# A transformer layer on one core: the pairs of scores as words of the plan, every engine's step in another order, and a chain of roots for each norm

## What is computed

```
h = segm_table[seg] + pos + token_table[tok]
x = layernorm(h)
q, k, v = split(x @ qkv_weight.T)              # 12 heads of 16
q = layer_norm(q) * 16 ** -0.5 ; k = layer_norm(k)
attn = softmax(einsum('bhnd,bhmd->bhnm', q, k))
h = h + (attn @ v) @ proj_weight.T
y = layernorm(h)
xq = round(clip(y / mean(alpha_a1), -8, 7)) ; wq1 = round(clip(w1 / alpha_w1, -8, 7))
x1 = clip(gelu(xq @ wq1.T * alpha_w1 * mean(alpha_a1) + b1), -10, 10)
hq = round(clip(x1 / mean(alpha_a2), -8, 7)) ; wq2 = round(clip(w2 / alpha_w2, -8, 7))
h = h + hq @ wq2.T * alpha_w2 * mean(alpha_a2) + b2
```

## Time and profile before

| | |
|---|---|
| median of 3 runs | 1070.74 us |
| lowest, highest | 1069.35, 1071.54 us |
| span of the profiled execution | 1067.6 us |
| PE busy | 979.4 us (92%) |
| ACT busy | 872.6 us (82%) |
| DVE busy | 813.9 us (76%) |
| POOL busy | 411.8 us (39%) |

### The profile page before, as it was taken

One profiled execution on the slowest core, in us unless ns is written; L12 is line 12 of the kernel. 1 busy time (PEld: TensorE's weight loads), 2 busy tenths in 40 slices (PEclk: granted clock), 3 DMA queues, 4 the chain that ended last, 5 costly groups with the idle time before them and its releaser, 6 DMA issues.

```text
span 1067.6 us, 19577 instructions
## 1 busy us (share of the span) xinstructions
PE 979.4 (92%) x7571; PEld 389.1 (36%) x7571; DVE 813.9 (76%) x2325; ACT 872.6 (82%) x950; POOL 411.8 (39%) x345
## 2 busy tenths in 40 slices
PE   5589999999999999999999999999999999989885
PEld 4333433334342433434343343434334343413223
DVE  5878869788686969878696977869697886825347
ACT  1387788897979889797988979798888989798883
POOL 6555513635343353534435363443526412201000
PEclk9899999999999999999999999999999999999997
DMA  7511200303011040202102040110202000000000
GB/s 162 127 16 16 31 1 2 46 1 64 12 25 22 1 75 1 38 8 58 18 2 45 1 73 3 31 16 16 30 1 45 1 16 1 16 1 1 16 1 31
DMA packets 25762, 28.62 MB, mean 27 GB/s; under 512 B 5027, under 2 KB 22182, under 8 KB 25670
## 3 DMA queue, kind: packets, MB, share of 16 engines
q0 software_dynamic: 16896, 11.80, 9.4%
q1 hardware_dynamic: 8624, 15.55, 4.8%
q10 hardware_dynamic: 150, 0.01, 0.0%
HBM read 21.06 MB, written 6.29 MB: 26 GB/s over the span
## 4 chain that ended last, share of the span: by engine, by line
PE 40%; ACT 30%; DVE 24%; issue 3%; POOL 3%; DMA 0%
ACT probs L682 22%; PE ps_o L1247 12%; PE ps_s L1227 8%; PE ps_j L1271 4%; ACT gelu L676 4%; PE ps_j L1279 3%; PE ps_j L1325 3%; POOL stack L592 3%; PE ps_j L1286 2%; PE ps_j L1292 2%; ACT L676 2%; ACT L682 2%; DVE hn L797 2%; PE ps_j L1311 2%; PE ps_j L1296 2%
## 5 line engine op out<-in xcount | busy, mean ns | idle before, releaser
L682 ACT ACTIVATE probs<-ps_s 128x1024 f32<-128x1024 f32 x768 | 736.1, 1023 | 125.5 <-PE ps_s L1227 120.6
L1247 PE MATMUL ps_o<-probs,v_sb 128*32 128x512 f32 x3072 | 394.7, 605 | 0.2 <-DVE o_sb L859 0.2
L1227 PE MATMUL ps_s<-qT,kT 64*128 64x512 f16 x1536 | 264.3, 384 | 35.0 <-ACT probs L682 25.2
L592 POOL TENSOR_TENSOR stack<-sq,stack 128x384 f16<-128x384 f32 x124 | 120.5, 992 | 162.9 <-DVE stack L846 162.9
L1227 PEld LDWEIGHTS ps_s<-qT,kT 64*128 64x128 f16 x1536 | 61.5, 93 | 299.5 <-ACT probs L682 267.6
L525 POOL DMA_INDIRECT h_all<-in_L_tok_token_table,idx x60 | 96.7, 1611 | 59.5 <-DMA h_all<-in_L_tok_segm_table,idx 41.2
L1247 PEld LDWEIGHTS ps_o<-probs,v_sb 128*32 128x32 f32 x3072 | 69.1, 109 | 124.3 <-issue 116.1
L601 POOL TENSOR_TENSOR y_sb<-y_sb,b_row 128x768 f32<-128x768 f32 x14 | 25.4, 1814 | 198.8 <-DVE y_sb L931 198.8
L581 POOL TENSOR_TENSOR sq<-qk 128x384 f32<-128x384 f32 x56 | 46.2, 826 | 139.5 <-DVE qk L894 139.5
L525 POOL DMA_INDIRECT h_all<-in_L_tok_segm_table,idx x56 | 87.2, 1557 | 15.2 <-issue 13.1
L1279 PE MATMUL ps_j<-wh,partsT 128*128 128x384 f16 (+1 forms) x384 | 71.5, 296 | 1.0 <-ACT partsT L663 0.7
(11 more groups left out here) (201 smaller groups left out, 1118.5 us busy)
## 6 DMA issues: line engine op xcount, KB each, us to landing
out<-h_all SPq DMA_DIRECT2D x15, 384.0 KB
h_all<-in_positions SPq DMA_DIRECT2D x7, 768.0 KB
gelu<-in_L_ffn_w SPq DMA_DIRECT2D x2, 576.0 KB
h_all<-in_L_tok_token_table,idx POOLq DMA_INDIRECT x60
h_all<-in_L_tok_segm_table,idx POOLq DMA_INDIRECT x56
probs<-in_L_attn_qkv_weight SPq DMA_DIRECT2D x2, 432.0 KB, 4.7
h_all<-in_positions SPq DMA_DIRECT2D x2, 384.0 KB, 8.0
o_nat<-in_L_ffn_alpha_a SPq DMA_DIRECT2D x1, 384.0 KB
```

The lines of the kernel that those rows point to most:

```text
L592: last = nc.gpsimd.tensor_tensor(low, src, high, ALU.subtract)
L682: nc.scalar.activation(probs[:, u % PROBS, 2 * pair:2 * pair + 2], ps_s[:, 2 * pair:2 * pair + 2], ACT.Exp, scale=SCORE_SCALE).then_inc(ex ...
L1227: last = mm(ps_s[:, j], kT[rows, par, head // 2, m * P:(m + 1) * P], qT[rows, par, head // 2, nh * NQ:(nh + 1) * NQ], start=True, stop=True)
L1247: last = mm(ps_o[32 * j:32 * j + 2 * D, :], v_sb[:, par, m, (GH * group + j) * VE:(GH * group + j) * VE + 2 * D], probs[:, u % PROBS, j], ...
```

## The change

PLAN is a new table. A new word s stands for one pair of scores; PE issues the pair and ACT its exp where the word stands, so the two pairs of a unit may have jobs or heads between them. There are still 48 pairs and 24 `h` in a step, and the same jobs; all stand in another order. New words give POOL its order from the same table: p and t (the two gathers), q (square of one tile), L (low parts of one tile), a (the result's addition). R is now the root of the first norm alone, and Q that of the second. N and m handle two tiles each, and come twice. W takes its bank by its number. DVE's n has a further wait, on the transposes of q. START_PLAN gets the words s (always as two at a line's head) and the words q and L at the end of step 0, which leaves its order as it was.

```diff
-Y0 Y1 Y2 F0 Y3 F1
-G0 F2 F3 H0 G1 P0
...
-C0 B0 X0
-X1 B1 r0 X2 X3 B2 X4 X5 r1 B3 h r2 h r3 g h
...
+s F0 F1 s p0 P0 h
+s G0 R0 G1 N0 F2 s h
...
+s h s n0 I2 Y1 n1 I3
+s s Y2 Y3 h E0 o X0 D0 X1 X2 g x0
+s X3 s x1 q2 X4 X5 n2 x2 q3 h h h C1 L0 D1 C2
...
+                for kind, t, at in step_work(s0):
+                    if kind == "a":
+                        add_result(s0, s)
+                    elif kind == "p" and FIRST_GATHERED <= ahead < HALVES:
+                        add_segments(ahead)
...
-            def norm_roots(s0):
-                lo = 0 if job_runs("P", s0) else 1
-                hi = 2 if job_runs("H", s0) else 1
-                if lo < hi:
-                    rsqrt(rn[:, lo:hi], vn[:, lo:hi], wn[:, lo:hi])
+            def norm_roots(which):
+                rsqrt(rn[:, which], vn[:, which], wn[:, which])
...
+                    dve.wait_ge(job_mm["D"], half * TH + (t - 1))
...
-                for j in range(GH):
-                    if j % 2 == 0 and (u or attends(s0 - 1)):
-
-                        pe.wait_ge(exp_done, 2 * UNITS * s + (2 * u - 1 + j // 2))
+                if u or attends(s0 - 1):
+
+                    pe.wait_ge(exp_done, 2 * UNITS * s + (2 * u - 1 + pair))
+                for j in (2 * pair, 2 * pair + 1):
```

More of the change, by code:

```diff
@@ L211, in bank_of @@
         return START_JOBS.index((job, s0)) % BANKS
-    return {"X": t % 2, "B": 2}[kind] if kind in "XB" else IN_TURN.index(job) % BANKS
+    return {"X": t % 2, "B": 2, "W": t % BANKS}[kind] if kind in "XBW" else IN_TURN.index(job) % BANKS
 def jobs_of(s0):
@@ L620, in _ @@
             add_segments(3)
-            split_low(-2, -2)
+            for t in range(TH):
+                split_low(-2, -2, t)
             add_tokens(2)
-            split_low(-1, -1)
+            for t in range(TH):
+                split_low(-1, -1, t)
             add_tokens(3)
@@ L685, in one @@
             def one(s0, s, b):
-                for u in range(UNITS):
-                    for kind, t, at in unit_work(s0)[u]:
-                        if kind in "abcd":
-                            copy_out(at, at, kind.upper(), t)
-                    if u == GELU_UNIT and job_runs("X", s0):
+                for kind, t, at in step_work(s0):
+                    if kind == "g" and job_runs("X", s0):
                         for j in range(HB):
                             gelu_out(s0, s, j)
-                    for pair in range(2):
-                        if attends(s0):
-                            exps(s0, s, u, pair)
+                    elif kind == "s" and attends(s0):
+                        exps(s0, s, t // 2, t % 2)
             for kind, t, s in FIRST_WORK:
@@ L795, in first_norm @@
                     dve.wait_ge(job_mm["A"], (s + 2) * TH)
-                for t in range(TH):
+                here = slice(0, TH) if s0 <= 0 else slice(2 * i, 2 * i + 2)
+                for t in range(TH)[here]:
                     last = ts(hn[:, t], h_tile(half, t), mv[:, 0, t, 0:1], rn[:, 0, t:t + 1],
@@ L1047, in one @@
             def one(s0, s):
[L1048 to L1059 removed]
+                for kind, t, at in step_work(s0):
+                    if kind == "o":
+                        if t == 0 and attends(s0 - 1):
+                            head_outputs(s0 - 1, s - 1, passes(s0 - 1) - 1)
+                        if t and attends(s0):
+                            head_outputs(s0, s, t - 1)
+                    elif at is None:
+                        work(s0, s, kind, t)
+                    elif kind not in "sh":
+                        work(at, at, kind, t)
             def step(ins):
```

215 lines of the change are left out of this document (102 added, 113 removed).

## The result

| | before | after |
|---|---|---|
| median | 1071.14 us | 1085.93 us |
| lowest, highest | 1069.35, 1071.54 us | 1080.95, 1086.38 us |
| span of the profiled execution | 1067.6 us | 1084.5 us |
| full steps (2 to 13), from the first exp to the next step's | 61.6 us | 62.2 to 62.3, five times 63.4 |
| step 1, which has the W jobs too | 63.4 us | 64.6 us |

The ratio after to before is 1.0134 (95% interval 1.0111 to 1.0157). The kernel before has a fourth run here, so its median is 0.4 us above that of the first table. The prediction was 1043 us, with 1024 to 1068 as its range: wrong in sign.

The account below looks back on a forecast made before the run. PE bounds the kernel, with 57.0 us of work in a 61.6 us step. From the 1070.7 us median, 13 full steps at 60.0 us give -20.8 and two light steps -7.0: 1043 us, range 1024 to 1068.

Parts of the forecast that it names:

- PE waits 3.7 us a step for exps; splitting the pairs takes them away: In PE's scores, 3.7 us of a full step is waiting for exps; an even spread regains that at most.
- The split costs 1.1 us of PE: In a full step, more runs of scores and jobs add 1.1 us, making PE's work 58.1 us.
- X jobs wait 1.7 us: At X2 to X5 behind the gelus, PE waits 1.7 us a step, between 0.7 and 3.0.
- The better rival: X's waits don't arise as scores and heads overlap more; full step 58.7 us, 1025 us in all; chance 0.13.
- POOL's moved addition costs 0: The result's addition, moved ahead of tile 2's low parts, costs 0, as POOL has 1 us to spare there.
- Both signs of being wrong: Long PE idle before q and k transposes, released by POOL or DVE; or granted clock under 1.00, 100 to 900 us.
- The slower rival: DVE, slowed beside POOL's addition, finishes n3 about 4.5 us late, delaying D3 and E3; 1077 us; chance 0.11.
- Its stated point of decision, 3.1 us at L3: The slower case decides from a delay of 3.1 us at L3 on: 1.5 spare plus 1.6 gained.
- The clock: At thin X jobs of full steps the granted clock falls, costing 1.1 us x 13; 1057 us; chance 0.06.
- Light steps: 54.4 us: The two last steps, without projections, take 54.4 us, 3.5 less each, -7.0 us together.
- Roots at 0: In DVE's queue, the second chain of roots adds 2.2 us a step but hides behind PE, costing 0.
- m0 done about 1 us before I0: In DVE's queue behind Q, m0 is finished about 1 us before job I0 on PE needs it.

Follow-up runs that it names:

- e8_old_short: The changed kernel's code with the order of before (1119 us), here with the second norm's roots cut to 2 of 11 instructions: 1089.20 us, ratio 1.0174.

## Why the prediction was wrong, step by step

**PE waits 3.7 us a step for exps; splitting the pairs takes them away.** Right. 3.8 before, 0.5 to 0.8 after, and 4.1 back when the pairs are put together.

**The split costs 1.1 us of PE.** Right: PE's work came to about 58.3 a step, predicted 58.1. The Trainium skill, TensorEngine Tiling (Array Packing), section Key Properties, has a drain at each change of the tiling mode. With 0.10 us a split from the row, the sum held to some 0.2 us for eleven more switches (58.3 is an estimate, the step less its waits), so no run here shows more of a drain than that.

**X jobs wait 1.7 us.** Too high; X and E0 together wait 0.8. The better rival, which had nothing here, was nearer, but its step of 58.7 us was never reached. The same plan with the addition elsewhere takes 59.97 us a step, where 60.0 stood in the sum. That agreement is partly luck: 0.9 too much here, and too little for m0 and the remaining waits for exps.

**POOL's moved addition costs 0; "POOL has 1 us to spare there".** This step failed. It asked whether POOL is in time and not what DVE loses beside it. x0 lost 2.5 us, C1's copy came that much later, and E1 waited 2 us. Moving it behind E3 took 62.25 - 60.62 = 1.6 us off a step, 12 x 1.6 = 20 us, and in five steps another 1.1 for the clock: 25 of the 27.5 us measured. The four places tried for one word give 1085.9, 1068.1, 1058.4 and 1053.0 us, so the place is worth 33 of the 43 us of the miss. Both signs of being wrong that the prediction named came: PE idle before a transpose of k, released by DVE, and a granted clock under 1.00 between 100 and 900 us.

**The slower rival** had the cause (DVE beside POOL's addition) and the sign, with 6 us slower where 15 were measured, but the wrong place: it looked to L3, D3 and E3, which held, and missed that C1's bank is E1's. It deserved more than 0.11: its price per instruction stood in the earlier trace rows, and only the walk through banks could say where it lands. Its stated point of decision, 3.1 us at L3, was not the one that decided.

**The clock.** The rival put it at the thin X jobs; it fell at E1 instead, behind PE's wait there. The length of one wait doesn't decide it: in the kernel with the addition ahead of tile 3's low parts, a single wait of 1.5 us a step was never followed by a fall, but in the old order with the short chain (e8_old_short) the clock fell in two full steps (at 586.2 and 838.8 us) behind waits of 0.35, 0.89 and 0.48 us close together. PE there, and the stretch behind, columns as above:

```profile
585.08 0.31 PE L1307 MATMUL ps_j<-ident_b,xq 128*96 128x128 bf16 x2 [0.89 <-ACT probs L686]
585.87 1.63 PE L1248 MATMUL ps_o<-probs,v_sb 128*32 128x512 f32 x8 [0.48 <-DVE o_sb L858]
```

```profile
586.00:588.00 2.00, 2.00 (x14) 0.58 (x10) 0.31 (x3) 0.00 (x0) 0.44 (x1) 0.56 0.52 50
```

Why it fell behind five of twelve equal waits in the changed kernel stays open.

**Light steps: 54.4 us.** Wrong: 58.7 and 59.2, in the best kernel still 57.9. ACT idles for 5.9 us of the first of them, 5.4 before, in pieces of up to 0.83 us:

```profile
954.90 1.94 ACT L686 ACTIVATE probs<-ps_s 128x1024 f32<-128x1024 f32 x2 [0.82 <-PE ps_s L1229]
...
963.81 4.77 ACT L686 ACTIVATE probs<-ps_s 128x1024 f32<-128x1024 f32 x5 [0.83 <-PE ps_s L1229]
```

The plan is even with A to E in it. When these jobs drop out, lines with F, G, H and X stay heavy, and the others leave PE waiting. That is read from the plan and these rows; no run tested it. I took the gain without walking the plan in that state. This is 8.6 us of the miss.

**Roots at 0.** Nearly right in the new order (0.4 us a step come back with nine of the eleven links left out, and I's wait goes), though "m0 done about 1 us before I0" was not: I0 waits 0.3 us. In the old order the same chain costs 40 us; the "2.3 us of PE without cover" of the prediction was a fair price there (2.9, with the clock).

**The sum again**, from the terms: full steps 817.3 - (802.1 - 20.8) = 36.0 over the forecast, light steps 117.8 - (116.2 - 7.0) = 8.6. That is 44.6 us. Step 1 has 2.8 of the 36.0: it was forecast 1.6 us faster and came out 1.2 slower. The prediction also took 3.1 us between span and median for launch and ends. Every run has 1.7 to 1.8 us there; the other 1.3 were that the profiled run was faster than the median. So 44.6 - 1.3 = 43.3 us are all of what lies between 1043 and the profiled run's 1086.3.

## What to carry to other kernels

Where PE is the bound and a plan is tightened, price each moved POOL instruction by the DVE instruction beside it, then follow DVE's queue to the first copy out of PSUM behind it and to the job that takes over that copy's bank. Slack of the moved engine says nothing about this. And an added chain has no price of its own: the same chain costs about 0.4 us a step or 2.9, by what stands behind it, so an edit and the order it comes with must be costed together.

## What the runs showed of the hardware

- A 128 by 512 fp32 elementwise instruction of DVE within SBUF takes 0.48 to 0.54 us alone and 1.58 to 1.94 beside a POOL addition of 1.8 us. In the rows shown with POOL's beside them it ends 0.3 us after POOL's. A copy out of PSUM keeps its 0.55 us there.
- Beside POOL's low parts the same instructions take 1.02 us.
- A wait of 2.1 us in a PE that was busy for 96% of the stretch was followed by a granted clock of half for 3.4 us, worth 1.1 us, in five of twelve steps. A single wait of 1.5 us a step wasn't, in any full step; waits of 0.35, 0.89 and 0.48 us close together were, in two.
- A small instruction suffers too: the second instruction of a chain of roots, 128 by 4, took 0.82 us beside POOL's square in all 13 full steps, where the same one of the other chain, without a square beside it, takes 0.17 in most (0.43 and 0.48 in two). In the changed kernel (DVE, Q, and POOL's square beside it):

```profile
520.28 0.16 DVE L745 TENSOR_SCALAR wn<-vn 128x4 int32<-128x4 int32 x1
520.48 0.82 DVE L746 TENSOR_SCALAR rn<-wn 128x4 int32<-128x4 int32 x1
```

```profile
520.45 0.83 POOL L580 TENSOR_TENSOR sq<-qk 128x384 f32<-128x384 f32 x1 [6.56 <-DVE qk L895]
```
